# Turning gathered embedding waves on VectorE with small DMAs instead of on TensorE, in a pairwise bilinear tower

## The reference

```python
e = jnp.stack([tbl_0[ids[:, 0]], ..., tbl_39[ids[:, 39]]], axis=1)     # 2048 x 40 x 32
out = jnp.einsum('bpd,pde,bpe->bp', e[:, iidx, :], bilinear_matrices, e[:, jidx, :])
h = jnp.concatenate([out, dense_ctx], axis=1)                          # 2048 x 796
h = jnp.maximum(h @ W_top1 + b_top1, 0.0)                              # 512
h = jnp.maximum(h @ W_top2 + b_top2, 0.0)                              # 256
y = h @ W_top3
```

## Time and profile before

| | us |
|---|---|
| median of 3 runs | 1245.42 |
| lowest and highest | 1243.78, 1253.85 |
| the profiled execution | 1242.61 |
| its span, first to last instruction | 1240.8 |
| TensorE busy with matmuls | 960.8 (77%) |
| VectorE busy | 549.1 (44%) |
| GpSimd busy | 475.7 (38%) |
| ScalarE busy | 173.9 (14%) |
| mean granted TensorE clock | 0.81 |

### The profile page before, as it was taken

One profiled execution on the slowest core, in us unless ns is written; L12 is line 12 of the kernel. 1 busy time (PEld: TensorE's weight loads), 2 busy tenths in 40 slices (PEclk: granted clock), 3 DMA queues, 4 the chain that ended last, 5 costly groups with the idle time before them and its releaser, 6 DMA issues.

```text
span 1240.8 us, 31357 instructions
## 1 busy us (share of the span) xinstructions
PE 960.8 (77%) x14536; PEld 473.6 (38%) x14536; DVE 549.1 (44%) x602; ACT 173.9 (14%) x432; POOL 475.7 (38%) x510
## 2 busy tenths in 40 slices
PE   4226779877887778787796878887788878888998
PEld 3012334333443234343243443443334423344556
DVE  4004345423654336443264443553335623355783
ACT  3011001011101111021010211012101121012211
POOL 7755342445233452434523434225442264322000
PEclk9557677778887879778887777878888878788999
DMA  4005100010000100001000010000100000000000
GB/s 143 14 13 180 34 10 6 10 35 10 6 8 8 35 10 6 9 9 35 11 6 8 8 34 10 6 7 14 32 10 6 6 13 10 8 7 6 4 3 2
DMA packets 24035, 24.54 MB, mean 20 GB/s; under 512 B 11173, under 2 KB 21217, under 8 KB 23777
## 3 DMA queue, kind: packets, MB, share of 16 engines
q0 software_dynamic: 15872, 8.16, 4.4%
q1 hardware_dynamic: 7418, 13.87, 3.4%
q10 hardware_dynamic: 616, 0.51, 0.1%
HBM read 22.44 MB, written 0.06 MB: 18 GB/s over the span
## 4 chain that ended last, share of the span: by engine, by line
PE 71%; issue 15%; another core or an unknown queue 10%; ACT 1%; DVE 1%; DMA 1%; POOL 0%; DVEq 0%; ACTq 0%
PE Y L614 23%; PE ZL L634 21%; PE ZL L660 13%; PE H L590 8%; PE H L573 3%; ACT xcols L742 1%; PE Y L669 1%; DVE prod L866 1%; DMA rows<-tbl,idx 0%; POOL rows L543 0%; PE Y L590 0%; PE Y L678 0%; PE ZL L640 0%; DMA idx<-ids 0%
## 5 line engine op out<-in xcount | busy, mean ns | idle before, releaser
L543 POOL DMA_INDIRECT rows<-tbl,idx x496 | 474.3, 956 | 652.5 <-PE H L573 472.3
L866 DVE TENSOR_TENSOR prod<-Y,xcols 128x1024 f32<-128x1024 f32 x352 | 419.3, 1221 | 538.0 <-remote 347.7
L634 PE MATMUL ZL<-prod,sel 128*32 128x256 f32 x3200 | 325.3, 432 | 48.3 <-issue 43.1
L614 PE MATMUL Y<-xcols,mats 32*64 32x256 f32 x6400 | 313.1, 434 | 29.3 <-ACT xcols L742 12.7
L614 PEld LDWEIGHTS Y<-xcols,mats 32*64 32x64 f32 x6400 | 162.6, 148 | 179.8 <-issue 132.0
L634 PEld LDWEIGHTS ZL<-prod,sel 128*32 128x32 f32 x3200 | 120.3, 120 | 194.9 <-issue 158.7
L660 PE MATMUL ZL<-z,w_sb 128*32 128x256 f32 x1568 | 162.8, 421 | 31.6 <-issue 30.0
L590 PE MATMUL H<-one,parts 125*32 125x256 bf16 x1560 | 97.7, 318 | 80.1 <-issue 80.0
L742 ACT ACTIVATE xcols<-H 32x256 f32<-32x256 f32 (+3 forms) x217 | 81.6, 376 | 546.1 <-PE H L573 335.0
L660 PEld LDWEIGHTS ZL<-z,w_sb 128*32 128x32 f32 x1568 | 66.9, 120 | 99.2 <-issue 73.8
L590 PEld LDWEIGHTS H<-one,parts 125*32 125x32 bf16 x1560 | 51.3, 104 | 128.9 <-issue 126.7
(11 more groups left out here) (43 smaller groups left out, 160.3 us busy)
## 6 DMA issues: line engine op xcount, KB each, us to landing
rows<-tbl,idx POOLq DMA_INDIRECT x496
idb<-ids_turned SPq DMA_DIRECT2D x8, 768.0 KB
w_sb<-w SPq DMA_DIRECT2D x1, 1792.0 KB
mats<-m_wide SPq DMA_DIRECT2D x1, 1152.0 KB
mats<-m_wide SPq DMA_DIRECT2D x1, 960.0 KB
mats<-m_wide SPq DMA_DIRECT2D x1, 768.0 KB, 6.3
tab<-tbl SPq DMA_DIRECT2D x6, 112.0 KB
w_sb<-w SPq DMA_DIRECT2D x1, 512.0 KB
```

Source lines behind the costliest of these rows:

```text
L543: pool.indirect_dma_start(out=rows[:, slot, t, D * q:D * (q + 1)], out_offset=None, in_=tables[f], in_offset=bass.IndirectOffsetOnAxis(ap= ...
L614: last = pe.matmul(Y[2 * D * c:2 * D * (c + 1), bank, cols], mats[D * r:D * (r + 1), u * P + 2 * D * c:u * P + 2 * D * (c + 1)], xcols[D * ...
L634: last = pe.matmul(Z[D * q:D * (q + 1), :], sel[:, GF * (SPAN - 1 - o):GF * (SPAN - 1 - o) + 32], prod[:, (2 * s + bank_of(k, q) // 2) % P ...
L866: dve.tensor_tensor(prod[:, half, :, :].rearrange("p b (u c) -> p b u c", c=BLK), Y[:, pair:pair + 2, :].rearrange("p b (u c) -> p b u c", ...
```

## The change

From block 2 on no gathered wave is turned by TensorE. VectorE transposes the gathered tile `rows` in squares of 32x32 (one instruction for a wave, a 128x256 tile) into a new ring `squares` of 4 waves. Then each quarter of `squares` holds, for every field, 32 dimensions on partitions and 64 samples; SyncE sends them to the right partitions of `xcols` with 16 small DMAs for each wave (4 fields x 4 quarters, 32 partitions x 256 bytes each). GpSimd's ring slot is free when VectorE has transposed it (`s_flip`). A second planner, `flip_steps`, names the step at whose end VectorE transposes each wave.

The order of samples in the columns of a block changes with this (`by_square`), and what still writes or reads columns follows. The third hot wave is looked up in blocks 0, 1, 2, 4 and 6. There are 62 gathered waves and 472 gathers then; 17 waves (blocks 0 and 1) are turned by TensorE and 45 by VectorE.

The diff, in its order: constants, planner, tiles, `place_squares` (SyncE), the wait ahead of a gather (GpSimd), the waits of `multiply`, `flip` (VectorE) and where it is called.

```diff
-ALL_HOT = (0, 4)
+ALL_HOT = (0, 1, 2, 4, 6)
+FLIP_RING = 4
+TURNED_LATE = 8
+def flipped(n, j):
+    return n > 1 or (n == 1 and j >= TURNED_LATE)
...
-    turns = [(n, j) for n in range(NB) for j in range(len(cold(n))) if ("turn", n, j) not in HEAD]
+    turns = [(n, j) for n in range(NB) for j in range(len(cold(n))) if not flipped(n, j) and ("turn", n, j) not in HEAD]
...
+START = 2700
+GATHERED, GATHER = 1500, 125
+PLACED = 900
+def flip_steps():
+    flips, total = [], 0
+    for n in range(NB):
+        for j, fields in enumerate(cold(n)):
+            total += BT * len(fields)
+            gs = {f // GF for f in fields}
+            first = min([need(fields)] + [max(mixed_at(k), 0) for k in MIXED if gs & {UNITS[u][0] for u in SLOTS[k]}])
+            flips.append((n, j, n * NS + first, GATHERED + GATHER * total))
+    at, now, v = {}, START, 0
+    for s in range(NB * NS):
+        for n, j, first, there in flips:
+            if first == s:
+                now = max(now, there + (PLACED if flipped(n, j) else 0))
+        while v < len(flips):
+            n, j, first, there = flips[v]
+            if flipped(n, j):
+                if s < (n - 1) * NS + 1 or (first > s + 1 and (there > now or s in at.values())):
+                    break
+                at[n, j] = s
+            v += 1
+        now += max(tensor_work(s), PRODUCTS)
+    return at
...
-        rows = sb("rows", [P, RING, BT, P], F32)
+        rows = sb("rows", [P, RING, GF, BT, D], F32)
+        squares = sb("squares", [P, FLIP_RING, GF, BT, D], F32)
...
+            def place_squares(v):
+                n, j = flips[v]
+                slot = v % FLIP_RING
+                sp.wait_ge(s_flip, v + 1)
+                if n > 1:
+                    sp.wait_ge(s_prod, 2 * (n - 1) * NS)
+                for f in cold(n)[j]:
+                    g, q = divmod(f, GF)
+                    for c in range(QUARTERS):
+                        sp.dma_start(xcols[D * q:D * (q + 1), n % 2, g, BT * D * c:BT * D * (c + 1)],
+                                     squares[D * c:D * (c + 1), slot, q, :, :]).then_inc(s_cols[slot], DMA)
...
-                    pool.wait_ge(s_turned, k - RING + 1)
+                    a = waves[k - RING]
+                    if flipped(*a):
+                        pool.wait_ge(s_flip, flips.index(a) + 1)
+                    else:
+                        pool.wait_ge(s_turned, k - RING + 1)
...
-                ready = [max(PASS[key] for key in sources(n, g)) + 1 for g in groups(w)]
-                pe.wait_ge(s_free, max(ready))
+                if passes_of(n, groups(w)) > 0:
+                    pe.wait_ge(s_free, passes_of(n, groups(w)))
+                seen = flips_of(n, {g for a in range(w) for g in groups(a)})
+                for v in flips_of(n, groups(w)):
+                    if v not in seen:
+                        pe.wait_ge(s_cols[v % FLIP_RING], cols_landed(v))
...
+            def flip(v):
+                n, j = flips[v]
+                slot, k = v % FLIP_RING, wave_number(n, j)
+                dve.wait_ge(s_rows[k % RING], landed(n, j))
+                if v >= FLIP_RING:
+                    dve.wait_ge(s_cols[slot], cols_landed(v - FLIP_RING))
+                dve.transpose(squares[:, slot, :, :, :].rearrange("p q t s -> p (q t s)"),
+                              rows[:, k % RING, :, :, :].rearrange("p q t d -> p (q t d)")).then_inc(s_flip, 1)
...
+                    for v in [v for v, wave in enumerate(flips) if FLIP_AT[wave] == n * NS + w]:
+                        flip(v)
```

59 lines of the change are left out of this document (40 added, 19 removed).

## The result

The changed kernel takes **1318.77 us** (median of 4 runs, 1317.85 to 1322.78), the kernel before 1249.63 (4 runs, 1243.78 to 1254.59): ratio **1.056 [1.050, 1.062]**, slower. The prediction was 1224 and faster. The profiled execution has a span of 1315.7 us at a mean granted clock of 0.781.

What follows compares the result with a forecast made beforehand. TensorE was taken as the bound, at its own rate and at a crawl during gather bursts; 1242.6 - 20.6 + 9.6 - 28.4 + 15.4 + 2.5 = 1221.1 us profiled, plus 2.8 gives 1224. Range 1192 to 1257.

Steps and rivals of the forecast that it cites:

- Item 7: SyncE's small DMAs beside TensorE: taken not to slow it as gathers do, 0, at most +9 us.
- Rival C: SyncE's transfers slow TensorE as gathers do, in a burst's first 3 us: 2.5 us a wave, 1336 us; chance 0.15.
- Item 6: SyncE's 720 small DMAs: 0.42 us each, 6.7 a wave; one late landing, +2.5 us, ends 0 and +10.
- Item 4: Gather bursts move to where VectorE's transposes release them, fewer in threes: 365.4 against 350.0 us, +15.4, ends -35.5 and +42.2.
- late landing: Block 3, the wave transposed at step (3, 7) and read in (3, 8): TensorE waits for its transfers, +2.5 us.
- Items 3 and 2: 24 fewer gathers, three bursts at 9.46 us: -28.4; third hot wave looked up in three more blocks: +9.6 us.
- rival E: TensorE's crawl has its own cause, and neither fewer nor moved gathers change it: 1234 us; chance 0.01.
- Item 5: VectorE's 45 transposes: 0.4 us each, taken as 0 for the total, upper end +18 us.
- Items 1 and 8: 48 fewer turns on TensorE at 0.43 us: -20.6; reordered columns and GpSimd's wait for the transpose: 0.
- Rival B: Evenly spread bursts are the dearest, 10.6 us each, with some late landings: 1256 us, 1240 with half; chance 0.19.
- A: Bursts standing alone cost no more than now, 9.46 us or less: 1208.6 us, or 1195 at 9.1; chance 0.20.
- D: The turns taken off TensorE weren't on the path, being done while it crawls: 1244 us; chance 0.03.

Runs made afterwards that it cites:

- e13: Changed kernel with transfers altered by block: half the bytes (2), gathers held until landing (3), 8 of 16 (4), no crossing of quarters (5): 1337.38 us, before 1252.28.
- e5: The changed kernel as it stands, timed again on another chip: 1311.12 us against 1229.64 for the kernel before, ratio 1.065.
- e12: The changed kernel with SyncE sending only 1 of a wave's 16 small transfers: 1226.74 us against 1233.04 for the kernel before, ratio 0.995.

## Why the prediction was wrong

**Item 7 failed** ("Do these DMAs slow TensorE like gathers? ... I take 0", with +9 as the upper end). In blocks 2 to 6 the transfers cost 64 to 71 us, nearly all of it as a deeper crawl. I had judged it by one `dpad` load beside TensorE with no gather near, and by that the zero was right: transfers alone cost nothing, in block 7 and at 712.5 us of e13. What I hadn't asked is what they do to a TensorE that is already slowed. The trace of before had no such overlap; the bound "by the nearest rows" should have come from the crawl, which was the only row of what a DMA can do to TensorE here. Rival C had that price (2.5 us a wave, 1336 us; measured 1.9 to 2.0 a burst, 1319), yet another place for it: the first 3 us of a burst, where TensorE was at full rate. Its sign came (fewer than 40 records in them; 38 in the burst above, 40 with one transfer), but the loss isn't mainly there. The records are 50.9 a burst in the first 3.5 us before, 45.6 with one transfer, 44.1 with all (e5) and 42.5 in the result (both without the stands), so most of that loss comes with the new places of the bursts; the loss by the transfers is in the 8 us behind, where two fifths of the records go.

**Item 6 was mis-sized.** A transfer takes SyncE 0.63 us or more, a wave 10.0 us or more, not 0.42 and 6.7; I took the price from loads of tables. With it the rule "two steps or more ahead is in time" failed: block 3 has two stands, not one, the added one for the wave transposed at the end of step (3, 4) and read in (3, 6). What they cost was small, though, as I had argued: TensorE would only have crawled. And I looked for waves that are read soon after their transpose, and not for a queue that is full: block 7, 15.7 us, was not in the sum at all, which had +2.5 for block 3. On kind F this is the whole result.

**Item 4 was too low, within its own ends.** Without transfers beside them bursts cost (728.1 - 373.4) / 34.9 = 10.2 us in e12, predicted 9.87, before 9.46, but e12 ran on a faster chip than the rows of before. By ratio, e12 is 0.995 [0.990, 1.000], and the prediction without its late landing 1221.5 / 1245.42 = 0.981: 17 us more than predicted (11 to 23). If all of it is item 4, this was nearer +32 than +15.4, with a stated upper end of +42. I had called this the likeliest place to fail.

**Items 3 and 2** hold together: six such waves gave -39.4 us for -42. That also rules out rival E, a crawl that doesn't follow the gathers. **Item 5**: 434 ns for 0.4. **Items 1 and 8** weren't tested alone and may share in the 17 us. Rival B, evenly spread bursts as the dearest kind, was right in direction, by about as much as its half (+13); A was wrong in direction; D wasn't tested.

So the parts are, in ratios that don't mix chips: e5 is 1.065 and e12 0.995, so the transfers cost 0.070 of 1230 us, some 86 us (64.5 of them in blocks 2 to 6 and 16 in block 7); the step from 0.981 to 0.995 is the 17 us above. Together that is 1.065 against 0.981; at the result it was 1.056, so chips of one kind differ by some 10 us in this. The split rests on e12 alone, one run on one chip, against two profiles of the change on two others.

## What to carry to other kernels

A transfer that is free beside a busy engine need not be free beside an engine that something else has already slowed: price an added DMA in the stretch where it will run, and if the trace has no row for that, keep the slowdown seen there as the upper end of the range. Work moved to many small DMAs is paid in the issuing queue, by their number and not their bytes; multiply it out per block against the shortest block there can be, and look for stretches in which the queue never empties. And when a cost hangs on the chip and not on the kernel, a change can win on one and lose on another; ask for both before building on it. Where chips of one kind differ as well, compare stretches of one trace, here the bursts ahead of the first transfer with those behind it.
